# Rotating the third rope chunk through a partition-swapped copy, in a one-core decoder block

## The reference, cut to what matters

```python
q_hk = (hidden_q @ Wq.T).reshape(Bv, Sv, H, K)               # 16 heads of 128
q_big = jnp.einsum('bshk,hkq->bshq', q_hk, w_kc_q)           # 16 heads of 192
q_big = q_big * cos + rotate_half(q_big) * sin               # halves of 96 exchanged
q_r = jnp.einsum('bshq,hqr->bhsr', q_big, W_qr)
k_r = jnp.einsum('bld,hdr->bhlr', rope(kv_c), W_kr)
scores = jnp.einsum('bhsr,bhlr->bhsl', q_r, k_r)             # then softmax, context, Wo
```

## Time and profile before

| | |
|---|---|
| median of 3 runs | 896.78 us |
| the profiled execution | 896.49 us |
| its span, first to last instruction | 894.7 us |
| PE (TensorE matmuls) busy | 844.7 us, 94% |
| DVE (VectorE) busy | 629.8 us, 70% |
| ACT (ScalarE) busy | 280.5 us, 31% |
| POOL (GpSimd) busy | 143.6 us, 16% |
| mean granted TensorE clock | 0.991 |

### The profile page before, as it was taken

One profiled execution on the slowest core, in us unless ns is written; L12 is line 12 of the kernel. 1 busy time (PEld: TensorE's weight loads), 2 busy tenths in 40 slices (PEclk: granted clock), 3 DMA queues, 4 the chain that ended last, 5 costly groups with the idle time before them and its releaser, 6 DMA issues.

```text
span 894.7 us, 14657 instructions
## 1 busy us (share of the span) xinstructions
PE 844.7 (94%) x5696; PEld 665.6 (74%) x5696; DVE 629.8 (70%) x1378; ACT 280.5 (31%) x502; POOL 143.6 (16%) x122
## 2 busy tenths in 40 slices
PE   5999999999999989999789989999999999999994
PEld 4977678776776767777568778788888888888873
DVE  3565787878878788788687776756575656566657
ACT  4531143212431124220353522332322333232232
POOL 2014400334013330133340400300000000000021
PEclk9999999999999999999999999999999999999997
DMA  9310000000001000000230004110212020000001
GB/s 337 118 36 2 1 2 1 21 29 17 1 1 48 2 16 1 0 25 4 83 105 0 25 25 154 42 59 1 89 48 65 0 88 27 31 1 1 1 24 71
DMA packets 12686, 35.84 MB, mean 40 GB/s; under 512 B 1488, under 2 KB 2384, under 8 KB 12112
## 3 DMA queue, kind: packets, MB, share of 16 engines
q1 hardware_dynamic: 12624, 34.98, 11.3%
HBM read 30.33 MB, written 2.36 MB: 37 GB/s over the span
## 4 chain that ended last, share of the span: by engine, by line
PE 81%; DVE 12%; issue 4%; ACT 2%; DMA 0%; POOL 0%; ACTq 0%; DVEq 0%
PE ps L243 20%; PE ps L244 19%; PE ps L245 19%; PE ps L1406 6%; PE ps L1486 5%; PE ps L1477 2%; PE ps L1288 2%; PE ps L1462 1%; PE ps L1324 1%; PE ps L1242 1%; DVE small L1090 1%; DVE x2T_all L500 1%; DVE su L508 1%; PE ps L1353 1%; PE ps L1281 1%
## 5 line engine op out<-in xcount | busy, mean ns | idle before, releaser
L508 DVE TENSOR_TENSOR su<-sg,ps 128x512 f32<-128x512 f32 x96 | 66.0, 687 | 131.6 <-PE ps L245 130.3
L243 PE MATMUL ps<-y_hi,f_hi 128*128 128x512 f32 x384 | 151.0, 393 | 0.0
L245 PE MATMUL ps<-y_hi,f_lo 128*128 128x512 f32 x384 | 149.5, 389 | 0.0
L244 PE MATMUL ps<-y_lo,f_hi 128*128 128x512 f32 x384 | 149.4, 389 | 0.0
L372 ACT ACTIVATE sg<-ps 128x512 f32<-128x512 f32 x96 | 57.3, 598 | 258.1 <-PE ps L245 258.1
L736 POOL TENSOR_TENSOR roped<-prod 128x512 f32<-128x512 f32 x64 | 80.9, 1286 | 174.5 <-DVE prod L1035 174.5
L1035 DVE TENSOR_TENSOR prod<-ps,ropeq 128x512 f32<-128x512 f32 x128 | 79.3, 681 | 27.7 <-PE ps L245 27.1
L244 PEld LDWEIGHTS ps<-y_lo,f_hi 128*128 128x128 f32 x384 | 72.1, 188 | 15.2 <-issue 0.5
L243 PEld LDWEIGHTS ps<-y_hi,f_hi 128*128 128x128 f32 x384 | 72.1, 188 | 15.2 <-issue 0.5
L245 PEld LDWEIGHTS ps<-y_hi,f_lo 128*128 128x128 f32 x384 | 72.1, 188 | 15.1
L243 PE MATMUL ps<-xT_hi,a_hi 128*128 128x512 f32 x192 | 78.6, 410 | 2.1 <-DVE xT_lo L960 2.1
(11 more groups left out here) (157 smaller groups left out, 1321.7 us busy)
## 6 DMA issues: line engine op xcount, KB each, us to landing
cb<-routing SPq DMA_DIRECT2D x32, 256.0 KB
f_raw<-in_L_ffn_gate_up_proj SPq DMA_DIRECT2D x8, 768.0 KB, 6.2
f_raw<-in_L_ffn_down_proj SPq DMA_DIRECT2D x8, 384.0 KB, 6.9
xb<-in_x SPq DMA_DIRECT2D x4, 512.0 KB, 4.1
lq<-in_L_xattn_Wq SPq DMA_DIRECT2D x1, 2048.0 KB, 15.2
x2T_all<-in_L_xattn_Wo SPq DMA_DIRECT2D x1, 2048.0 KB, 9.0
x2T_all<-x2T SPq DMA_DIRECT2D x4, 512.0 KB, 3.2
out<-res SPq DMA_DIRECT2D x4, 512.0 KB, 2.6
```

The lines of the kernel that those rows point to most:

```text
L243: pe.matmul(dst, l_hi, r_hi, start=first, stop=False, skip_group_check=check)
L244: pe.matmul(dst, l_hi, r_lo, start=False, stop=False, skip_group_check=check)
L245: return pe.matmul(dst, l_lo, r_hi, start=False, stop=last, skip_group_check=check)
L508: dve.tensor_tensor(su[:, k % 2], sg[:, k % 2], bank(2 * (k % 2) + 1), ALU.mult).then_inc(s_su, 1)
```

## The change

The third chunk is rotated like the other two. ScalarE copies it from PSUM into a new tile, swap, with the 32-partition quarters exchanged (0 with 1, 2 with 3): four copies of 32 x 512 per pair. VectorE multiplies this copy in place by the sin table, and the PSUM chunk by the cos table; GpSimd adds the two. latent_q has three chunks, not four, and waits for a third add; m_w and the raw W_qr have three chunks, not four.

The order of the q_big chunks on TensorE becomes 2, 0, 1, so that the copy can start early, but for the pairs 1, 2 and 3 of blocks 1 to 3, where it stays 0, 1, 2 (chunk 2 waits there for other users of its bank). VectorE's first product of a pair then waits for all three chunks, and for two only in those pairs. The copies of pair p+2 stand in ScalarE's list behind its copy of latent query p; those of the pairs 0 and 1 at the head of the stage.

```diff
-    m_w = sb(att, "m_w", [P, PAIRS, 4 * DC])
+    m_w = sb(att, "m_w", [P, PAIRS, 3 * DC])
...
+    swap = sb(att, "swap", [P, 2, BT])
...
+    swap_last = lambda later, p: later and p in (1, 2, 3)
+    chunk_order = lambda later, p: (0, 1, 2) if swap_last(later, p) else (2, 0, 1)
...
                     pool.tensor_tensor(roped[:, p % 2, k], prod[:, 2 * k], prod[:, 2 * k + 1], ALU.add)\
                         .then_inc(s_rope, 1)
+                pool.wait_ge(s_rp, 24 * b + 3 * p + 3)
+                pool.tensor_tensor(roped[:, p % 2, 2], roped[:, p % 2, 2], swap[:, p % 2], ALU.add).then_inc(s_rope, 1)
...
+            def swap_out(p):
+
+                act.wait_ge(s_q, 24 * b + 3 * p + (3 if swap_last(later, p) else 1))
+                if b or p >= 2:
+                    act.wait_ge(s_rope, 24 * b + 3 * p - 3)
+                for i in range(4):
+                    j = i ^ 1
+                    ins = act.activation(swap[32 * i:32 * i + 32, p % 2], ps[32 * j:32 * j + 32, 3 * (p % 2) + 2, :], ACT.Copy)
+                ins.then_inc(s_sw, 1)
+
+            swap_out(0)
             act.wait_ge(s_x1, 4 * b + 4)
             if later:
                 x2T_out(b - 1, 2, 5)
             else:
                 act.activation(x1[:], xn[:], ACT.Copy).then_inc(s_x1c, 1)
+            swap_out(1)
...
+                if p + 2 < PAIRS:
+                    swap_out(p + 2)
...
                     if k < 2:
                         if p >= 1:
-                            dve.wait_ge(s_rope, 16 * b + 2 * p - 1 + k)
-                        dve.wait_ge(s_q, 24 * b + 3 * p + 2)
+                            dve.wait_ge(s_rope, 24 * b + 3 * p - 2 + k)
+                        dve.wait_ge(s_q, 24 * b + 3 * p + (2 if swap_last(later, p) else 3))
                         times(prod[:, 2 * k], f + k, 2 * k)
                         times(prod[:, 2 * k + 1], f + 1 - k, 2 * k + 1).then_inc(s_rp, 1)
                     else:
                         if p >= 2:
                             dve.wait_ge(s_qr, 8 * b + p - 1)
-                        dve.wait_ge(s_q, 24 * b + 3 * p + 3)
-                        times(roped[:, p % 2, 2], f + 2, 4)
-                        times(roped[:, p % 2, 3], f + 2, 5).then_inc(s_rp, 1)
+                        dve.wait_ge(s_sw, 8 * b + p + 1)
+                        rotated = t64(swap[:, p % 2])
+                        dve.tensor_tensor(rotated, rotated, ropeq[:, 5, :].unsqueeze(1).broadcast_to((P, SEQS, SEQ)), ALU.mult)
+                        times(roped[:, p % 2, 2], f + 2, 4).then_inc(s_rp, 1)
...
-                for k in range(4):
-                    if k < 2:
-                        pe.wait_ge(s_rope, 16 * b + 2 * p + k + 1)
-                    elif k == 2:
-                        pe.wait_ge(s_rp, 24 * b + 3 * p + 3)
+                for k in range(3):
+                    pe.wait_ge(s_rope, 24 * b + 3 * p + k + 1)
                     for h in range(2):
                         for th in range(2):
...
-                for k in range(3):
+                for k in chunk_order(later, p):
```

More of the change, by code:

```diff
@@ L124, in build @@
     x2f = x2T_all[:, :, :].rearrange("p c n -> p (c n)")
-    l_qr = x2f[:, 0:2048].rearrange("p (r k n) -> p r k n", r=PAIRS, k=4)
+    l_qr = x2f[:, 0:1536].rearrange("p (r k n) -> p r k n", r=PAIRS, k=3)
     r_kr = x2f[:, 2048:2560].rearrange("p (r n) -> p r n", r=PAIRS)
@@ L198, in build @@
     s_q, s_rp, s_rope = sem("q_big_in_psum"), sem("rope_products_ready"), sem("roped_ready")
+    s_sw = sem("halves_swapped")
     s_qr, s_lq = sem("latent_q_in_psum"), sem("latent_q_ready")
@@ L652, in _ @@
             sp.dma_start(raw_w[i], a[name]).then_inc(s_raw0[i], 16)
-        sp.dma_start(x2f[:, 0:2048], a["L0_xattn_W_qr"]).then_inc(s_raw2, 16)
+        sp.dma_start(x2f[:, 0:1536], a["L0_xattn_W_qr"]).then_inc(s_raw2, 16)
         sp.dma_start(x2f[:, 2048:2560], a["L0_xattn_W_kr"]).then_inc(s_raw2, 16)
@@ L1071, in shift @@
             if t == 0:
-                dve.wait_ge(s_rope, 16 * b + 16)
+                dve.wait_ge(s_rope, 24 * b + 24)
             if t >= 2:
@@ L1406, in latent_q @@
                             mm = pe.matmul(ps[r:r + 64, q_bank(p, h), 0:256], m_w[i, p, k * DC:(k + 1) * DC],
-                                           roped[i, p % 2, k, 256 * th:256 * th + 256], start=k == 0, stop=k == 3)
+                                           roped[i, p % 2, k, 256 * th:256 * th + 256], start=k == 0, stop=k == 2)
                 mm.then_inc(s_qr, 1)
@@ L1419, in pairs @@
                     pe.wait_ge(s_rp, 24 * b + 3 * p - 3)
+                    pe.wait_ge(s_sw, 8 * b + p - 1)
                 if later and p == 2:
@@ L1586, in _constants @@
                      np.concatenate([cos[:, high], cos[:, high + HALF]], 1),
[L1587 removed]
+                     np.concatenate([-sin[:, high], sin[:, high + HALF]], 1)])
     c["ropeq"] = np.ascontiguousarray(np.tile(rows.transpose(2, 0, 1), (2, 1, 1))).astype(f)
@@ L1601 @@
     tiles = lambda w: w.reshape(-1, P, w.shape[-1]).transpose(1, 0, 2)
-    order = np.r_[0:64, 96:160, 64:96, 160:192, 160:192, 64:96]
+    order = np.r_[0:64, 96:160, 64:96, 160:192]
     lay = {
@@ L1608 @@
         "L0_xattn_Wq": tiles(x["L0_xattn_Wq"]),
-        "L0_xattn_w_kc_q": x["L0_xattn_w_kc_q"][:, :, order[0:DQ]].transpose(1, 0, 2),
+        "L0_xattn_w_kc_q": x["L0_xattn_w_kc_q"][:, :, order].transpose(1, 0, 2),
         "L0_xattn_w_kc_kv": x["L0_xattn_w_kc_kv"].transpose(1, 0, 2),
-        "L0_xattn_W_qr": x["L0_xattn_W_qr"][:, order].reshape(PAIRS, 2, 4 * 64, 64).transpose(1, 3, 0, 2)
-                         .reshape(P, PAIRS * 4 * 64),
+        "L0_xattn_W_qr": x["L0_xattn_W_qr"][:, order].reshape(PAIRS, 2, 3 * 64, 64).transpose(1, 3, 0, 2)
+                         .reshape(P, PAIRS * 3 * 64),
         "L0_xattn_W_kr": x["L0_xattn_W_kr"].reshape(PAIRS, 2, DC, 64).transpose(1, 3, 0, 2).reshape(P, PAIRS * DC),
```

4 lines of the change are left out of this document (2 added, 2 removed).

## The result

| | before | after |
|---|---|---|
| median | 896.63 us (4 runs) | 918.03 us (4 runs) |
| ratio | | 1.0248 (95%: 1.0235 to 1.0261) |
| the profiled execution | 896.49 us | 919.26 us |
| its span | 894.7 us | 917.5 us |
| mean granted TensorE clock | 0.991 | 0.972 |

The change makes the kernel 21 us, 2.5%, slower, though it takes 288 instructions from TensorE. The forecast was 913.4.

What follows compares the result with a forecast made beforehand. VectorE was taken to bound blocks 1 and 2 behind pair 3, TensorE block 0's pairs. Blocks 0 to 3 and fold_m: 0.9 + 6.7 + 6.7 + 3.7 - 1.1 = 16.9, on 896.5: 913.4 us, range 901.5 to 920.5.

Steps and rivals of the forecast that it cites:

- The shared side: VectorE instructions with two SBUF inputs and GpSimd's wait for each other, 1.13 us at most each time for VectorE's small ones.
- D(p): The time at which VectorE starts its first product of pair p.
- D(3) to D(4): Block 1: waits of 1.05 for the copy, 0.25 for an add, 0.77 in `route`, less 0.36 idle: +1.7 us.
- Rival 2: Only the large instructions wait for GpSimd: +6.3 - 1.1, 901.7 us; chance 0.11.
- rivals 1 and 3: 1: TensorE keeps setting the pace, 881.6 us, chance 0.07; 3: no waits on the shared side, 897.2 us, chance 0.06.
- rival 4: GpSimd is served first when both wait, so multiplications wait for the second add too: 920 to 934 us; chance 0.10.
- Rival 5: latent_q keeps its length, as TensorE isn't paid by the instruction; time as forecast, counted there without its own chance.
- The new order: Chunks 2, 0, 1: VectorE's first product waits for all three, 1.36 us later, not hidden at the stage's start.
- the tail: From D(7) to the last latent query copy: 6.81 us, +1.3 in blocks 1 and 2, +0.9 in blocks 0 and 3.
- the gaps: Stretches between the stages `pairs`: forecast 0, as a shift of a stage's last copy was a shift of the kernel.
- TensorE idle ahead of L(6) and L(7): Sign that the forecast is right: TensorE waits ahead of latent_q of pairs 6 and 7; no size given.
- The `fold_m` term: Ahead of the first stage: a quarter of `fold_m`'s 128 instructions goes, -1.1 us (0 to 1.2), with nothing hiding it.

Runs made afterwards that it cites:

- The idle add: The kernel before with one more GpSimd add per pair, between constant SBUF tiles, for which nobody waits: 903.14 us, 1.0083.
- the multiplication from PSUM: The changed kernel with the sin multiplication reading the PSUM chunk, not the swapped copy in SBUF; copy, waits and third add stay: 909.42 us, 1.0154.
- filler: The changed kernel with unused matmuls ahead of waits of latent_q in blocks 1 to 3: 918.89 us; with fewer of them in block 3: 917.31 us.

## Why the prediction was right, and by what it was short

Direction, mechanism and place were right; the time was 4.6 us short.

**The shared side.** D(p) of block 1, from the stage's start: D(3) +1.01 (forecast 0.93), D(3) to D(4) +1.72 (1.7), D(4) to D(5) +1.43 (1.4), D(5) to D(6) +1.24 (1.25), D(6) to D(7) +0.12 (0.1). The idle add showed that the small instructions' waits come from what the two engines share and not from data, and cost 2.6 us in each of the blocks 1 and 2; the multiplication from PSUM, that its place is worth 8.6 us over the kernel. Rival 2 (only large instructions wait) fell by L1170's 1.14 us on four columns; rivals 1 and 3 with it; rival 4 (GpSimd served first) by the multiplications of 0.81 us and GpSimd's two adds of 3.00 where 2.53 was usual. Rival 5 has its answer too: block 0's pair went from 6.24 to 5.77 us, and from a latent_q's first matmul to the next chunk's it takes 1.45 us (72.03 to 73.48) for 1.89. So latent_q did become shorter, by 0.44, near the 0.43 of the forecast, and the pair by 0.47.

**A sum that was right with a wrong part.** D(3) to D(4): I had a wait of 1.05 us for ScalarE's copy and 0.25 for an add (I wrote the first; at D + 3.45 it is the second that runs in my own schedule). The row has 1.30 of idle and a multiplication of 0.69, without a wait. I had taken four copies as 2.0 us, spaced 0.48 as the two at 436.69; they take 2.40, 0.60 each:

```profile
190.21 2.40 ACT L839 ACTIVATE swap<-ps 32x512 f32<-32x512 f32 x4 [2.80 <-PE ps L249]
```

By the time of the later copy both adds had all but passed (190.29 to 192.82, the multiplication starts at 192.71). The two errors cancel, which the sum alone wouldn't have shown.

**The new order** was priced well at D(0) (+1.38 for 1.36). In the run with the order alone it cost 6.9 us, in the changed kernel undoing it returned 2.9.

**The mis-sized term: the tail.** From D(7) to the last copy I forecast 6.81 us; all four stages show 7.21 or 7.22. The adds ran as forecast (the third ended at D + 5.96, I had 6.1); the last third of latent_q took 1.13 us for 0.66, at the lower clock. Over four stages 1.7 us. Where the clock stayed up and no more than two filler matmuls stood in the way it was 6.79 and, without filler in block 0, 6.74. Another 0.6 of the stages are small excesses of D(7), 0.26 in block 0.

**The missing term: the gaps.** I took a shift of a stage's end as a shift of the kernel and put nothing on the stretches between. They carry 3.9 us in the profiled execution, and there the lower clock shows: TensorE, which before came out of each stage at full clock, comes out of waits of 0.6 to 0.9 us ahead of each third. "TensorE idle ahead of L(6) and L(7)" stood in the forecast as a sign; that the idle could have a price beyond its own length did not. How well the stalls are shown to be the cause differs by place. The gaps behind blocks 1 and 2 (0.6 and 0.4 us) went back with filler in both runs. The 1.1 us behind block 0 were gone in one execution that had the same waits and no filler there. The 1.85 us behind block 3 are within what that stretch varies by in kernels without these stalls (458.75 to 461.24).

**The `fold_m` term** was sized well, and the 1.42 us ahead of the first stage are only in part its own. From its first matmul to the first one behind it, it takes 3.88 us (17.35 to 21.23) for 4.91 (17.70 to 22.61): 1.03 for the forecast's 1.1. Another 0.35 is a start that came 0.35 earlier, with the clock up 1.36 us sooner; with the order alone, where `fold_m` is as before, the first stage began at 56.78 for 57.70. Together, the profiled execution against the forecast's 16.9: 3.9 + 1.7 + 0.6 - 0.3 = 5.9, which is the profile's 22.8.

What stays open is how much of this the median carries, and what else than the stalls moves the clock. With the filler one execution was 3.6 us shorter (1.1 of it in the gap behind block 0, where no filler stood, and 1.4 behind the last stage), the median 0.7.

## What to carry to other kernels

Before work is given to an idle engine, ask which engine has to wait while it runs: 1.3 us of GpSimd's time on SBUF can cost VectorE 1.1 us in a four-column instruction, and it costs the end wherever VectorE has no slack. Ask the gain pair by pair, since the same edit gained 0.47 us per pair in block 0, where TensorE set the pace, and 4.8 us over the kernel where only 12 pairs of 32 were rotated, and lost the kernel 21 us when it was made everywhere. And where a change makes TensorE wait several times in a row, look at the granted clock of the stretch behind it, in more than one execution: the same waits were followed by a low clock in one and not in another.

## What the runs showed of the hardware that I had not expected

- Four ScalarE copies of 32 partitions from one bank into the exchanged quarters of a tile follow each other every 0.60 us, with no overlap (2.40 for four), where two others of that shape took 1.06 together. What keeps them apart wasn't tried.
- A TENSOR_SCALAR with one SBUF input of four columns waits for GpSimd as the two-input ones do (1.14 us at L1170); one of a single column (0.15 at 175.08) and a RECIPROCAL on the tile of L1170 (0.18 in the middle of an add) don't. The Trainium skill ("VectorE: DVE Perf Modes", section "Mode 2×_2P — use both read ports for one tensor") has it that a float32 TENSOR_SCALAR within SBUF uses both read ports for its one tensor, which it splits in half. The rows agree: the four columns wait, the single one doesn't.
- Six waits of TensorE in a row, of 0.6 to 0.9 us, were accompanied or followed by stretches at a mean clock of 0.55 to 0.81: eight matmuls took 0.5 us longer, and the stretches up to the next stage 0.4 to 1.1 us. Five waits of the same lengths in block 0 of another execution left the clock at 1.00.
